# A graph and expert network on one core: the second edge layer, its feed-forward and the experts in one instruction stream

## The reference

```python
x = x + L0_gnn(ln(x))   # edge layer 1: gather rows by src, sum by dst, two 256x256 products, unit length
x = x + L0_ffn(ln(x))   # 256 -> 1024 (gelu) -> 256, kept for the 3124 nodes of largest router weight
x = x + L1_gnn(ln(x))   # edge layer 2, cut below
x = x + L1_ffn(ln(x))   # 8 experts, cut below

# L1_gnn
h = (xn @ W).reshape(N, 8, 32)
e = leaky_relu(a_src[src] + a_dst[dst], 0.2)           # src, dst with one self loop per node
alpha = exp(e - max_by_dst) / sum_by_dst
out = layer_norm(segment_sum(h[src] * alpha, dst) + xn @ W_res + bias)
return out + gelu(out @ ffn_w1 + b1) @ ffn_w2 + b2     # 256 -> 1024 -> 256

# L1_ffn
w = softmax(x @ Wr + br)                               # 8 shares per node
h = relu(bn(x @ W1[e])); h = relu(bn(h @ W2[e])); y = h @ Wo[e] + bo[e]
return sum_e w[:, e] * y                               # every node goes through all 8 experts
```

## Time and profile before

| | us |
|---|---|
| median of 3 runs | 3651.28 |
| profiled execution, whole | 3654.82 |
| its span, first to last instruction | 3653.5 |
| TensorE busy in the span | 3153.1 (86%) |
| VectorE, ScalarE, GpSimd busy | 2063.8 (56%), 1363.5 (37%), 1634.8 (45%) |
| mean granted TensorE clock | 0.916 |

### The profile page before, as it was taken

How to read it: one execution, slowest core, us unless ns; L and a number is a source line. 1 busy time by engine, 2 the same in 40 slices (tenths; PEclk the granted TensorE clock), 3 DMA queues, 4 the chain that set the end, 5 groups by cost and what they waited for, 6 DMA issues and landing times. The chain is left out here.

```text
span 3653.5 us, 51694 instructions
## 1 busy us (share of the span) xinstructions
PE 3153.1 (86%) x18956; PEld 2769.3 (76%) x18956; DVE 2063.8 (56%) x5102; ACT 1363.5 (37%) x2634; POOL 1634.8 (45%) x1623
## 2 busy tenths in 40 slices
PE   8378998988888547689999999999869999999999
PEld 7256876877777447578888888888758888888888
DVE  9645554555545476556665666656446555555554
ACT  0012332332324224123333332332435666566666
POOL 0377777777774012577767777777200000000000
PEclk9888998999999668699999999999969999999999
DMA  2433333333332014343333333333111000000000
GB/s 81 147 103 103 103 101 103 103 101 103 103 103 65 1 58 123 94 111 108 106 105 105 104 104 106 105 102 101 46 37 41 7 7 12 7 7 7 7 12 8
DMA packets 151429, 269.21 MB, mean 74 GB/s; under 512 B 52170, under 2 KB 99772, under 8 KB 151164
## 3 DMA queue, kind: packets, MB, share of 16 engines
q0 software_dynamic: 75168, 211.78, 20.6%
q1 hardware_dynamic: 72540, 50.73, 4.6%
q10 hardware_dynamic: 3456, 3.26, 0.3%
HBM read 238.76 MB, written 26.89 MB: 73 GB/s over the span
## 5 line engine op out<-in xcount | busy, mean ns | idle before, releaser
L1483 POOL DMA_INDIRECT G<-tab,SRCL x784 | 822.0, 1049 | 326.0 <-issue 263.9
L604 POOL DMA_INDIRECT G<-tab,SRCL x782 | 771.7, 987 | 379.9 <-issue 366.8
L1510 PE MATMUL PB<-WG,OR 128*128 128x264 f32 x1568 | 423.3, 417 | 18.1 <-DVE WG L1616 17.9
L1995 ACT ACTIVATE TFm<-PB,BIA,SCL 128x512 f32<-128x512 f32 (+1 forms) x416 | 313.8, 754 | 253.4 <-PE PB L94 253.1
L624 PE MATMUL PB<-G,OR 128*128 128x257 f32 x782 | 272.5, 433 | 139.3 <-DMA G<-tab,SRCL 117.2
L1510 PEld LDWEIGHTS PB<-WG,OR 128*128 128x128 f32 x1568 | 309.1, 206 | 71.8 <-DVE WG L1616 21.2
L2029 DVE TENSOR_TENSOR H2l<-TFm,H2h 128x512 fp32r<-128x512 f32 (+1 forms) x208 | 137.7, 662 | 272.1 <-ACT H2h L2000 271.9
L624 PEld LDWEIGHTS PB<-G,OR 128*128 128x128 f32 x782 | 136.2, 208 | 193.0 <-DMA G<-tab,SRCL 168.6
L625 PE MATMUL PB<-G,OR 128*128 128x257 f32 x782 | 258.3, 414 | 0.0
L1616 DVE TENSOR_TENSOR WG<-G,WG 128x1024 f32<-128x1024 f32 x196 | 238.9, 1219 | 1.7
L708 DVE TENSOR_TENSOR OR<-iotaf,REL 128x256 f32<-128x256 f32 x391 | 163.3, 421 | 134.4 <-PE PB L625 122.5
(11 more groups left out here) (327 smaller groups left out, 8570.5 us busy)
## 6 DMA issues: line engine op xcount, KB each, us to landing
G<-tab,SRCL POOLq DMA_INDIRECT x1566, 2.8
tab<-ACC SPq DMA_DIRECT2D x7, 896.0 KB, 5.5
resd<-RSG SPq DMA_DIRECT2D x49, 128.0 KB, 1.8
RI<-resd SPq DMA_DIRECT2D x49, 128.0 KB
tab<-ACC SPq DMA_DIRECT2D x12, 512.0 KB, 3.2
out_x<-X SPq DMA_DIRECT2D x12, 512.0 KB
MWs<-in_L_ffn_W SPq DMA_DIRECT2D x16, 256.0 KB, 2.7
X<-in_x SPq DMA_DIRECT2D x4, 896.0 KB, 16.8
```

Of the source, the lines that this page charges most:

```text
L604: po.indirect_dma_start(b.G[:, u % RU, q, 0:256], None, c.tab0, bass.IndirectOffsetOnAxis(ap=c.SRCL[:, 2 * u + q:2 * u + q + 1].bitcast(U3 ...
L1483: po.indirect_dma_start(b.G[:, j % RP, u, :], None, c.tab1, bass.IndirectOffsetOnAxis(ap=c.SRCL[:, 4 * j + u:4 * j + u + 1].bitcast(U32), ...
L1510: ins = pe.matmul(PB[3 + w % 2][:, 0:264], b.OR2[:, j % 4, u, :].bitcast(F32), b.WG[:, j % 2, u, :], start=(first and u == 0), stop=(last ...
L1995: a.activation(b.TF[:, m, 0:n], PB[2 + 2 * l + m][:, 0:n], ACT.Relu, bias=b.BIA[:, l, q:q + 1], scale=b.SCL[:, l, q:q + 1]).then_inc(relu, 1)
```

## The change

It has three parts.

1. The expert weights are split once, in `prep`: SyncE loads each of the 24 pieces, ScalarE casts the high half, GpSimd subtracts the low half, SyncE stores both (512 KB) in DRAM as `msplit`.
2. `attend` also writes `x` to DRAM (`xd`), and no longer weights the tiles by their self loops. `X` and `ACC` end there.
3. `second_layer` and `experts` become one stage, `last_layers`. The tiles form 14 groups: two of 2 tiles, eleven of 4, one of 1. In step s of `last_plan` three lists are merged by written costs: the edge units of group s, the node steps (feed-forward, router) of group s-1, and the 8 expert steps of group s-2. Rows of `tab1`, `x` and the residual come from DRAM into rings of 12 tiles, and every weight piece is fetched again for every group, into a ring of `RQ` = 7 slots. PSUM is dealt anew: the hidden tiles, expert layers and router products take turns on banks 3, 4 and 6 (`ROUND`), all output products of the experts use bank 7, all windows bank 2, and the factor products share bank 1 with the tiles' sums.

```diff
+LGROUPS = [[0, 1], [2, 3]] + [list(range(4 * g, 4 * g + 4)) for g in range(1, 12)] + [[48]]
+ROUND = (3, 4, 6)
+RQ = 7
+RX = 12
+RA = 12
+RS = 4
 # prep
+def prep_sp_weights(sp, c, b, S, A):
+    for n in range(24 + 2):
+        if n < 24:
+            if n >= RS:
+                sp.wait_ge(S.w_lo, n - RS + 1)
+            sp.dma_start(b.MWs[:, n % RS, :].rearrange("p (k n) -> p k n", k=2), expert_piece(A, n)).then_inc(raw_in(S, n), 16)
+        if n >= 2:
+            sp.wait_ge(S.w_lo, n - 1)
+            sp.dma_start(c.msplit[n - 2], ...)
+def prep_act_weights(a, b, S):
+        a.copy(b.MWS[:, n % RS, 0, :], b.MWs[:, n % RS, :]).then_inc(S.w_hi, 1)
+def prep_pool_weights(po, b, S):
+        po.tensor_tensor(b.MWS[:, n % RS, 1, :], b.MWs[:, n % RS, :], b.MWS[:, n % RS, 0, :].bitcast(F32),
+                         ALU.subtract).then_inc(S.w_lo, 1)
 # prep_sp: after the loads of x
+    prep_sp_weights(sp, c, b, S, A)
     for i in range(7):
         sp.wait_ge(S.table, i + 1)
         sp.dma_start(t0v[:, 7 * i:7 * i + 7, :], c.ACC[:, 7 * i:7 * i + 7, :]).then_inc(S.tab0_out, 16)
 # attend_sp, after the store of a group's table
+            sp.wait_ge(S.bias, t[-1] + 1)
+            sp.dma_start(xdv[:, t[0]:t[-1] + 1, :], c.X[:, t[0]:t[-1] + 1, :]).then_inc(S.xd_out, 16)
 # attend_dve, at its end
-    on.wait_ge(S.tab1_out, 16 * 14)
     own.done(v.tensor_tensor(c.DEN[:, :, :], b.AD[:, :, 0:8], b.AD[:, :, 8:16], ALU.max))
-    for k in range(NT):
-        hk = ACC[:, k, 0:256].rearrange("p (h d) -> p h d", h=8)
-        ins = v.tensor_tensor(hk, hk, c.DEN[:, k, :].unsqueeze(2).to_broadcast([P, 8, 32]), ALU.mult)
 # the merged list
+def node_stream(g):
+    yield ("fetch_x", g), 0.0, ()
+    ...
+    yield ("turn_rows", h), 0.5, (("rows_lo", h),)
+    for z in range(8 * nh + 1):
+        hh, m = divmod(z, 8)
+        if z < 8 * nh:
+            yield ("hidden", h + hh, m), 0.8, (("ht_lo", h + hh, m),)
+        if z:
+            yield ("output", h + (z - 1) // 8, (z - 1) % 8), 0.8, ((("taken", h + hh - 1),) if m == 0 else ())
+    ...
+    for s in range(7):
+        yield ("prepare", g, s), 0.9, ()
+def expert_stream():
+    parts = [[] for _ in LGROUPS]
+    for it in range(NI + 1):
+        p = parts[min(it // 8, len(LGROUPS) - 1)]
+        ...
+        if old:
+            layer(it - 1, 1, 0)
+            layer(it - 1, 1, 1)
+        if new:
+            layer(it, 0, 0)
+        if old:
+            output(it - 1, 0)
+        if new:
+            layer(it, 0, 1)
+        if old:
+            output(it - 1, 1)
+def last_plan(fast):
+    for s in range(len(LGROUPS) + 2):
+        lists = [
+            [(x, c, ()) for x, c in edges[s]] if s < len(edges) else [],
+            list(node_stream(s - 1)) if 1 <= s <= len(LGROUPS) else [],
+            experts[s - 2] if s >= 2 else [],
+        ]
+        ...
+            i = min((i for i in range(3) if at[i] < len(lists[i])), key=lambda i: done[i] / whole[i])
 # last_sp
+        elif step == "weights":
+            q, piece, key = x
+            if q >= RQ:
+                piece_read(on, S, *slots[q - RQ])
+            sp.dma_start(b.MW[:, q % RQ, :, :].rearrange("p a n -> p (a n)").bitcast(F32), c.msplit[piece]).then_inc(piece_in(S, q), 16)
 # last_pe, the experts' outputs
+            q = weights(it, 2)
+            bank(7)
+            ...
+            free[7] = (S.out_add, ADDED[it, h, len(tiles) - 1])
 # second_layer: before both_ways; now last_consts_sp in the body, with the experts' small tables
-    nc.scalar.wait_ge(S.consts, 48)
+        last_consts_sp(nc.sync, b, S, A)
```

More of the change, by code:

```diff
@@ new lines, in needed_by, with with_weights @@
+def needed_by(step, x, late):
+    if step == "layer":
+        return x[1] == 1 and late[:3] == ("h_lo", x[0], 0)
+    if step == "products":
+        return late[:3] == ("h_lo", x[0], 1) or late[0] == "out_add"
+    return late[0] == "out_add"
+def with_weights(plan):
+    uses = []
+    for n, (step, *x) in enumerate(plan):
+        if step == "layer" and x[2] == 0:
+            uses.append((n, 3 * (x[0] % 8) + x[1], (x[0], x[1])))
+        elif step == "products" and x[1] == 0:
+            uses.append((n, 3 * (x[0] % 8) + 2, (x[0], 2)))
+    at = {}
+    for q, (n, piece, key) in enumerate(uses):
+        at.setdefault(uses[q - RQ + 1][0] if q >= RQ - 1 else 0, []).append(("weights", q, piece, key))
+    out = []
+    for n, x in enumerate(plan):
+        out.extend(at.get(n, ()))
+        out.append(x)
+    return out
@@ new lines, in rounds_of @@
+def rounds_of(plan):
+    bank, turn = {}, 0
+    for step, *x in plan:
+        keys = []
+        if step in ("turn_rows", "hidden", "layer"):
+            keys = [(step, *x)]
+        elif step == "prepare":
+            g, s = x
+            if s == 1:
+                keys = [("prepare", g, 1, 0), ("prepare", g, 1, 1)]
+            elif s in (2, 4) or s in (5, 6) and LGROUPS[g][2 * (s - 5):2 * (s - 5) + 2]:
+                keys = [("prepare", g, s)]
+        for y in keys:
+            bank[y] = ROUND[turn % len(ROUND)]
+            turn += 1
+    return bank
@@ new lines, in piece_slots, with added_counts, last_added, last_alloc @@
+def piece_slots(plan):
+    return {key: q for step, *x in plan if step == "weights" for q, piece, key in [x]}
+def added_counts():
+    n, at = 0, {}
+    for it in range(NI):
+        for h in range(2):
+            for i in range(len(LGROUPS[it // 8][2 * h:2 * h + 2])):
+                n += 1
+                at[it, h, i] = n
+    return at
+ADDED = added_counts()
+def last_added(it):
+    tiles = LGROUPS[it // 8]
+    return ADDED[it, (len(tiles) - 1) // 2, (len(tiles) - 1) % 2]
+def last_alloc(nc, sb):
@@ L1453, in second_sp, with last_sp @@
+def last_sp(nc, c, b, S, plan, fast, out):
+    sp = nc.sync
     on = Awaited(sp)
+    rdv, xdv = nodes(c.resd), nodes(c.xd)
+    own_rows = nodes(c.tab1) if fast else nodes(c.accd)
     first = []
+    slots = [key for step, *x in plan if step == "weights" for q, piece, key in [x]]
     for step, *x in plan:
[L1456 to L1461 removed]
+        if step == "window":
@@ L1593, in second_dve @@
         onehot(0)
+    last_dve_consts(v, on, own, b, S)
     for step, *x in plan:
```

1174 lines of the change are left out of this document (608 added, 566 removed).

## The result

The changed kernel takes 3740.98 us, median of 4 runs (3728.09 to 3748.78), against 3655.39 us (median of 4, 3650.65 to 3660.56) for the kernel before on the same chip: a ratio of 1.023, 95% interval 1.0195 to 1.0266. It is slower, by 2.0 to 2.7%; 3570 us had been forecast, and the range ended at 3665. The profiled execution took 3744.5 us, its span is 3740.4 us.

What follows compares the result with a forecast made beforehand. GpSimd's gathers were taken to set the second edge layer's pace, with TensorE filling the experts. 3654.8 + 20 (split) - 12 (`attend`) + 3 (storing `x`) - 94 (merge) = 3572, predicted as 3570 us; range 3495 to 3665.

Steps and rivals of the forecast that it cites:

- Part 1: First stage, split of the expert weights: GpSimd's subtractions hold VectorE up, +20 us (bounds 10 to 39).
- Part 2: End of `attend`: self-loop weightings leave it, -12 us; storing `x` delays the residual rows, +3 us (0 to 12).
- Part 3: Merged stage, from the second layer's first gather to the end: 2077 us against 2171, -94 us.
- TensorE's work: Merged stage: units, feed-forward and tile sums 955 us at full clock, an expert step 9.0 us; 1852 in all.
- The clock: Merged stage: the real clock costs 4% on TensorE's counted work, 76 us.
- Idleness: Merged stage: TensorE idle for 149 us in all.
- The start: Merged stage's first three steps, with too little work beside gathers and node chain: 34, 17 and 6 us lost.
- The stalls in the merge: Merged stage: stalls of 4.5% over some 1630 us, 73 us, and 8 us in the last full group's steps.
- Rival C: Merged stage: VectorE's order and bank 7 stretch the experts' chain, 2.0 us a step, 3687 us; chance 0.19.
- Rival D: Merged stage stalls as the edge layer did, 10% with its clock, 3660 us, no change; chance 0.09.
- Rival E: Weight streaming: pieces come at half of 348 GB/s, last tile 9 us a step, +40, 3610 us; chance 0.08.
- Rival B: Merged stage as dense as the experts: stalls 1%, first stage 5 us, 3498 us; chance 0.17.

Runs made afterwards that it cites:

- e6: Changed kernel with GpSimd's 24 first-stage subtractions on 8 of 512 columns: 3940.0 us, 0.968 of the kernel before, second kind of chip.
- e7: Changed kernel with TensorE's last-tile waits filled by products into a bank nobody reads: 3971.4 us, 0.976 of the kernel before, second kind of chip.
- e2: Changed kernel with the experts' output products alternating between PSUM banks 6 and 7: 3690.5 us, 1.010 of the kernel before.
- e1: Changed kernel with the first six weight pieces issued after the first windows of factors: 3728.5 us, 1.020 of the kernel before.
- e5: Changed kernel with four residual-row buffers instead of two, asked for four tiles ahead: 3957.7 us, 0.974 of the kernel before, second kind of chip.
- e17: Changed kernel with two output banks, windows first, four residual buffers, weight split moved, tile sums in output banks, later additions, filled last-tile waits: 3611.7 us, 0.988.
- e4: Changed kernel loading only the first 7 of 336 weight pieces, used by all experts: 3703.5 us, 1.013 of the kernel before.
- e11: The same kernel as e17, on the second kind of chip: 3899.7 us, 0.946 of the kernel before.
- e16: The same kernel as e17, once more on the second kind of chip: 3897.6 us, 0.950 of the kernel before.
- e13: The kernel before, unchanged, profiled on the second kind of chip: 4073.8 us in one run.

## Why the prediction was wrong

- **Part 1** was right: 24.0 us against 20, by the mechanism named (e6).
- **Part 2** was right: from GpSimd's last addition to `X` in `attend` to the first gather 24.1 us instead of 39.1, -15 against -12. The stores of `x` cost 3.6 against 3: from the last gather of the first layer to that addition 294.0 us against 290.4.
- **Part 3** was wrong, 2248.5 us against 2077, and with it the sign. By its own terms, in the columns of the first table:
  - *TensorE's work* ("955 us at a full clock", an expert step 9.0 us, in all 1852) is the step that failed by most: 1931 us, 79 short. The kernel before has 1928 by the same measure, 1015 up to 2716 where 955 had been counted, 885 among the experts where 869 had. The earlier trace rows show it without any window: TensorE was busy for 1034.9 + 63.7 us with the part priced at 993. So of the "235 us to win" 76 were never there: with this term put right and all else as forecast the sum is 3572 + 76 = 3648 us, no change. Which products the count left out is not worked out.
  - *The clock* (76 us) was 126. 4% was put on all work; the first three steps have 0.85, the last tile 0.54, and the middle steps fall to half behind waits like the one at 2256 above.
  - *Idleness* (149 us) was 191.5. The start (34 + 17 + 6 = 57) was right with 52.6, though a third of it is a cause that I had not followed, the windows behind 3 MB of pieces in SyncE's queue. The stalls in the merge (73 and 8) were 106 + 20 = 126 us, 6.3% of the middle steps, inside the 3 to 7% that I had allowed. The last tile was to idle for 11 us and idled for 12.6; it took 59 us instead of 39 for its clock, and in part for the order of its products (e7).
- In all: 79 + 50 + 42 = 171 us. Of these the bank (e2), the windows (e1), the residual rows (e5) and the clock of the last tile (e7, e17) are shown by runs; the work is shown by traces alone: in the middle steps it is 1515 to 1519 us in the changed kernel and in all six other runs of the first kind, whose idleness there goes from 66 to 109 us. So it does not follow the waits.
- **Rival C** named the mechanism on the slower side: VectorE's order and the single bank 7. It was right in kind, e2 gives 40 to 53 us for it. But it was priced as 2 us in each of 96 steps, and it comes in 25 places with 1.5 us each and the clock behind them. Its sign, an expert step of over 20 us, did come (1688.5 / 80 = 21.1 us), but 19.0 of these are work. C had 0.19 and ended at 3687.
- **Rival D** (stalls as in the edge layer, 10% with the clock) gave 3660. The middle steps did lose 10% so (106 us idle and 65 of clock in 1688.5), but not to gathers.
- **Rival E** (streaming) was right that streaming costs, wrong in how: not bytes, but residual rows queued behind pieces whose slots are not free (e4, e5).
- **Rival B** (as dense as the experts) fell: even with all mends the middle steps are idle for 4% (66 of 1616.6 us).
- The forecast had no word on where the kernel runs. On the second kind the gathers are slower, and what the weave gives is more than its losses.

## What to carry to other kernels

Before the work of an engine is counted from start to start, compare the count with its busy time times the granted clock in the trace of the kernel before: here the count was 76 us short, and no weave could have given them. Before several chains are woven into one in-order stream, follow each PSUM bank and each queue to the instruction that frees it, and look what stands ahead of that instruction: here one bank emptied behind another chain's wait cost 40 to 53 us, and small loads behind large ones 14 to 29. A wait of TensorE costs more than its idle time where the clock falls behind it, so take the clock from a stretch with the same waits, not from the average. A weave that hides gathers also makes a kernel less dependent on how fast they are; that can be worth more than the median on one chip shows.

## What the runs showed of the hardware

- The granted clock fell to 0.54 over the last tile of the changed kernel (3681 to 3740), where TensorE never waited longer than 0.9 us, though the same products ran at 0.96 in the kernel before, with waits of 0.35 us where the changed kernel has 0.56 to 0.87. Filling the waits with idle products held it at 0.92 to 0.93 (e7, e11, e16, e17) and gave 13 us with 5 of them a step. The Trainium skill ("TensorE: Matmul & The Clock Gate", section "A second HAM failure mode: psum-queue depth-cycling") tells of a kernel whose clock swung because TensorE idled briefly but often between groups of products. The last tile agrees in the cause, but its clock did not swing: it stayed at 0.50 from 3690 to 3740.
- The kernel before takes 3650 us in some places and 4067 to 4123 in others, and the difference lies in the two stages with gathers, none of it among its experts (e13).
- Behind a unit's eight sums in float32 the first product of another kind holds the engine 0.43 us, from its start to the next, instead of 0.23 (2805.24 above).
